# Products of a 128-deep contraction cut into row halves of TensorE and run in pairs

## What is computed

```python
Kf  = einsum('bjd,ed->bje', F, K_w)      # K's product, contraction over d = 128
S   = einsum('bid,bjd->bij', F, Kf)      # scores
out = einsum('bij,ijd->bid', S, W)       # one 64 x 128 matrix W[i] for each row i
out = out + einsum('bid,ed->bie', F, Q_w)  # Q's product, contraction over d = 128
```

## Time and profile before

| What | us |
|---|---|
| median of 3 runs (607.74 to 608.13) | 607.75 |
| the profiled execution, its own time | 608.0 |
| its span | 606.2 |
| PE busy | 597.5 |
| PE weight loads busy | 527.0 |
| VectorE busy | 398.7 |
| ScalarE busy | 401.5 |

### The profile page before, as it was taken

One profiled execution on the slowest core, in us unless ns is written; L12 is line 12 of the kernel. 1 busy time (PEld: TensorE's weight loads), 2 busy tenths in 40 slices (PEclk: granted clock), 3 DMA queues, 4 the chain that ended last, 5 costly groups with the idle time before them and its releaser, 6 DMA issues.

```text
span 606.2 us, 17908 instructions
## 1 busy us (share of the span) xinstructions
PE 597.5 (99%) x7693; PEld 527.0 (87%) x7693; DVE 398.7 (66%) x412; ACT 401.5 (66%) x698; POOL 0.2 (0%) x4
## 2 busy tenths in 40 slices
PE   9999999999999999999999999999999999999995
PEld 7888989889898898988889898898988989889894
DVE  6556757567685665947659475686756768567376
ACT  7978393874938659295692947839387493865830
POOL 0000000000000000000000000000000000000000
PEclk9999999999999999999999999999999999999998
DMA  8543847548575575755647566385755757457177
GB/s 324 239 141 145 322 169 282 199 177 312 189 281 173 212 262 208 280 200 208 246 183 284 204 248 241 140 322 173 285 197 186 304 196 282 173 211 259 66 279 278
DMA packets 29452, 137.60 MB, mean 227 GB/s; under 512 B 3264, under 2 KB 4032, under 8 KB 21312
## 3 DMA queue, kind: packets, MB, share of 16 engines
q1 hardware_dynamic: 20592, 75.38, 31.5%
q10 hardware_dynamic: 8784, 61.08, 28.4%
HBM read 69.34 MB, written 67.11 MB: 225 GB/s over the span
## 4 chain that ended last, share of the span: by engine, by line
PE 98%; DVE 1%; issue 1%; DVEq 0%
PE ps L501 20%; PE ps L440 20%; PE ps L442 19%; PE ps L441 19%; PE ps L527 18%; DVE o_sb L371 1%; PE ps L557 1%; DVEq L46 0%; PE ps L457 0%; PE ps L461 0%; PE ps L459 0%; DVE o_sb L380 0%; DVE f_hi L385 0%
## 5 line engine op out<-in xcount | busy, mean ns | idle before, releaser
L336 DVE TENSOR_TENSOR f_lo<-f_ring,f_hi 128x1024 fp32r<-128x1024 f32 x124 | 151.8, 1224 | 169.6 <-ACT f_hi L214 167.9
L228 ACT ACTIVATE q_out<-ps 128x512 f32<-128x512 f32 x256 | 156.9, 613 | 6.4
L219 ACT ACTIVATE kf<-ps 128x512 f32<-128x512 f32 x256 | 155.9, 609 | 3.4
L371 DVE TENSOR_TENSOR o_sb<-ps,q_out 128x1024 f32<-128x1024 f32 x127 | 145.1, 1213 | 19.3 <-PE ps L527 19.3
L237 ACT ACTIVATE s_t<-ps 128x512 f32<-128x512 f32 x32 | 19.1, 598 | 176.5 <-PE ps L501 176.5
L501 PE MATMUL ps<-f_ring,kf 128*64 128x64 f32 x4096 | 124.1, 222 | 0.4 <-issue 0.4
L501 PEld LDWEIGHTS ps<-f_ring,kf 128*64 128x64 f32 x4096 | 121.6, 138 | 2.9 <-issue 0.8
L527 PEld LDWEIGHTS ps<-s_t,w_sb 64*128 64x128 f32 x2048 | 115.6, 188 | 5.6 <-issue 5.6
L527 PE MATMUL ps<-s_t,w_sb 64*128 64x128 f32 x2048 | 118.6, 274 | 0.0
L440 PE MATMUL ps<-f_hi,k_hi 128*128 128x512 f32 x254 | 100.7, 397 | 0.0
L440 PE MATMUL ps<-f_hi,q_hi 128*128 128x512 f32 x256 | 99.9, 390 | 0.0
(11 more groups left out here) (36 smaller groups left out, 164.3 us busy)
## 6 DMA issues: line engine op xcount, KB each, us to landing
out<-o_sb SPq DMA_DIRECT2D x127, 512.0 KB, 3.5
f_ring<-f_t ACTq DMA_DIRECT2D x58, 1024.0 KB, 4.8
f_ring<-f_t SPq DMA_DIRECT2D x4, 1024.0 KB, 10.4
w_sb<-w SPq DMA_DIRECT2D x1, 2048.0 KB, 18.8
f_ring<-f SPq DMA_DIRECT2D x6, 256.0 KB, 5.1
out<-o_sb SPq DMA_DIRECT2D x2, 256.0 KB, 2.4
f_ring<-f SPq DMA_DIRECT2D x3, 128.0 KB, 2.6
f_ring<-f ACTq DMA_DIRECT2D x1, 128.0 KB, 4.3
```

Source lines behind the costliest of these rows:

```text
L219: nc.scalar.activation(kf[:, c // 2, c % 2 * CK:(c % 2 + 1) * CK, :, :].rearrange("d k h i -> d (k h i)"), ps[:, 2 * c % 8, :], COPY).then ...
L228: nc.scalar.activation(q_out[:, t % 2, :, :].rearrange("d i (h b) -> d i h b", h=2)[:, :, :, at:at + CK], q_bank(t * CHUNKS + c).rearrange ...
L336: nc.vector.tensor_tensor(f_lo[:, v % SPLIT, :], f_unit(v), f_hi[:, v % SPLIT, :].bitcast(F32), ALU.subtract).then_inc(flo_done, 1)
L371: nc.vector.tensor_tensor(o_sb[:, n % OBUF, :, :], ps[:, bank:bank + 2, :], q_out[:, t % 2, :, :].rearrange("d (s m) b -> d s (m b)", s=2) ...
```

## The change

Every product is cut over d into two halves of 64 rows. In a step, a half of one product runs on the lower rows of TensorE and a half of another on the upper rows, pass by pass in turn: first Q's lower half beside K's upper half (`first_halves`), and later K's lower half beside Q's upper half (`second_halves`). The second halves of chunk n are issued after the first halves of chunk n+1. Each pair of passes writes two banks. The second halves wait until the first halves of the same step are complete (`half_done`). The last two chunks are handled as two steps: K's two products side by side, and, after the last scores, Q's two. The first two chunks stay as they were.

K's and Q's products of a chunk now end together, so the users of the slots of `f_hi` and `f_lo` wait for both `q_done` and `k_done`, and TensorE waits for both copies of the chunk four earlier before its first halves. `FILL` is larger.

```diff
-FILL = {2: 58}
-FILL.update((t, 108) for t in range(3, TILES - 1))
-FILL[TILES - 1] = 132
+FILL = {1: 235}
+FILL.update((t, 220 + t % 2) for t in range(2, TILES - 1))
+FILL[TILES - 1] = 284
...
                 act.wait_ge(q_done, 2 * (v - SPLIT) + 2)
+                act.wait_ge(k_done, 2 * (v - SPLIT) + 2)
                 nc.scalar.activation(f_hi[:, v % SPLIT, :], f_unit(v), COPY).then_inc(fhi_done, 1)
...
                 dve.wait_ge(q_done, 2 * (v - SPLIT) + 2)
+                dve.wait_ge(k_done, 2 * (v - SPLIT) + 2)
                 nc.vector.tensor_copy(f_hi[:, v % SPLIT, :], f_unit(v)).then_inc(fhi_dve, 1)
...
-            def k_product(c):
-                three(ps[:, 2 * c % 8, :], k_hi, k_lo, f_hi[:, c // 2 % SPLIT, piece_cols(c)],
-                      f_lo[:, c // 2 % SPLIT, piece_cols(c)]).then_inc(k_done, 1)
+            def products(step):
+                n = min(step, TILES * CHUNKS - LATE)
+                if step < TILES * CHUNKS - LATE:
+                    return (q_of(n), q_done), (k_of(n), k_done)
+                if step == n:
+                    return (k_of(n), k_done), (k_of(n + 1), k_done)
+                return (q_of(n), q_done), (q_of(n + 1), q_done)
...
+            def passes(dst, w_hi, w_lo, c, rows, first):
+                hi = f_hi[rows, c // 2 % SPLIT, piece_cols(c)]
+                lo = f_lo[rows, c // 2 % SPLIT, piece_cols(c)]
+                yield nc.tensor.matmul(dst, w_hi[rows, :], hi, start=first, stop=False)
+                yield nc.tensor.matmul(dst, w_hi[rows, :], lo, start=False, stop=False)
+                yield nc.tensor.matmul(dst, w_lo[rows, :], hi, start=False, stop=not first)
+
+            def first_halves(step):
+                (a, _), (b, _) = products(step)
+                for ins_a, ins_b in zip(passes(*a, lower, True), passes(*b, upper, True)):
+                    pass
+                ins_a.then_inc(half_done, 1)
+                ins_b.then_inc(half_done, 1)
+
+            def second_halves(step):
+
+                pe.wait_ge(half_done, 2 * (step - 1))
+                (a, a_sem), (b, b_sem) = products(step)
+                for ins_b, ins_a in zip(passes(*b, lower, False), passes(*a, upper, False)):
+                    pass
+                ins_b.then_inc(b_sem, 1)
+                ins_a.then_inc(a_sem, 1)
...
-                        pe.wait_ge(kf_copied, n - 3)
+                        k_pieces = 2 if n == TILES * CHUNKS - LATE else 1
+                        pe.wait_ge(kf_copied, n - 4 + k_pieces)
+                        if k_pieces == 1:
+                            pe.wait_ge(q_copied, n - 3)
                     elif t >= 1:
 
                         pe.wait_ge(s_copied_act if c % 2 else s_copied, (t - 1) * 2 + c // 2 + 1)
-                    k_product(n)
-                    if c >= 4:
-                        pe.wait_ge(q_copied, n - 3)
-                    if t < TILES - 1 or c < CHUNKS - LATE:
-                        q_product(n)
+                    first_halves(n)
+
+                    if c >= 1 and n > 2:
+                        second_halves(n - 1)
                     for x in range(FILL.get(t, 0) * c // CHUNKS, FILL.get(t, 0) * (c + 1) // CHUNKS):
                         pe.wait_ge(zeros_done, 1)
+                second_halves(min((t + 1) * CHUNKS - 1, TILES * CHUNKS - LATE))
...
-                    for c in range(CHUNKS - LATE, CHUNKS):
-                        q_product(t * CHUNKS + c)
+                    first_halves(TILES * CHUNKS - LATE + 1)
+                    second_halves(TILES * CHUNKS - LATE + 1)
```

More of the change, by code:

```diff
@@ L92, in build @@
         fhi_done, flo_done = sem("fhi_done"), sem("flo_done")
+        half_done = sem("half_done")
         k_done, kf_copied = sem("k_done"), sem("kf_copied")
@@ L205, in split_first @@
                 wait(act, q_done, 2 * (c // 2 - SPLIT) + 2)
+                wait(act, k_done, 2 * (c // 2 - SPLIT) + 2)
                 nc.scalar.activation(f_hi[:, c // 2 % SPLIT, piece_cols(c)], f_cols(c), COPY).then_inc(fhi_first, 1)
@@ L213, in split_f @@
                 act.wait_ge(q_done, 2 * (v - SPLIT) + 2)
+                act.wait_ge(k_done, 2 * (v - SPLIT) + 2)
                 nc.scalar.activation(f_hi[:, v % SPLIT, :], f_unit(v), COPY).then_inc(fhi_done, 1)
             def copy_kf(t, c):
-                act.wait_ge(k_done, t * CHUNKS + c + 1)
+                n = t * CHUNKS + c
+                act.wait_ge(k_done, n + 1 if n < TILES * CHUNKS - LATE else TILES * CHUNKS)
                 nc.scalar.activation(kf[:, c // 2, c % 2 * CK:(c % 2 + 1) * CK, :, :].rearrange("d k h i -> d (k h i)"),
@@ L222, in copy_q @@
             def copy_q(t, c):
-                act.wait_ge(q_done, t * CHUNKS + c + 1)
+                n = t * CHUNKS + c
+                act.wait_ge(q_done, n + 1 if n < TILES * CHUNKS - LATE else TILES * CHUNKS)
                 if c == 0:
@@ L327, in both_first @@
                 wait(dve, q_done, 2 * (c // 2 - SPLIT) + 2)
+                wait(dve, k_done, 2 * (c // 2 - SPLIT) + 2)
                 if c == 4:
@@ L442, in three, with k_of, q_of @@
                 return nc.tensor.matmul(dst, w_lo[:, :], hi, start=False, stop=True)
-            def k_product(c):
-                three(ps[:, 2 * c % 8, :], k_hi, k_lo, f_hi[:, c // 2 % SPLIT, piece_cols(c)],
-                      f_lo[:, c // 2 % SPLIT, piece_cols(c)]).then_inc(k_done, 1)
+            def products(step):
[5 more added lines that the diff above has]
+                return (q_of(n), q_done), (q_of(n + 1), q_done)
+            def k_of(c):
+                return ps[:, 2 * c % 8, :], k_hi, k_lo, c
+            def q_of(c):
+                return q_bank(c), q_hi, q_lo, c
+            def passes(dst, w_hi, w_lo, c, rows, first):
[17 more added lines that the diff above has]
+                ins_a.then_inc(a_sem, 1)
             def q_product(c):
@@ L467, in project @@
                     n = t * CHUNKS + c
+                    if n == TILES * CHUNKS - 1:
+                        break
                     if n < 2:
```

## The result

The changed kernel takes 614.61 us (median of 4 runs, 613.15 to 615.43), the kernel before 607.75 us beside it. The ratio is 1.0113, with a 95% interval of 1.0088 to 1.0138: slower by 6.9 us, where 2.4% less was predicted. The profiled execution took 613.15 us, with a span of 611.4 us, 5.2 more than before.

A forecast was written before the change was run, and what follows sets the result against it. TensorE's products and the seams between stages were taken as the bound. The span was 606.2 - 12.8 - 2.9 + 0.9 + 0.2 = 591.6 us, and 591.6 + 1.8 - 0.25 gave 593.2 us, range 586 to 601.

The forecast's parts named there:

- The pair's pitch: In the products, a pair of row halves takes 0.2183 us instead of 0.2267 for a full matmul: 12.8 us gained.
- row of 256-column pieces: Pieces at 0.12 us each, 0.013 over their 0.107: the excess is a fixed amount for each matmul, not a slower stream.
- Work costed at nothing because it runs ahead: In TensorE's queue, doubled weight loads and 220 filling waits a tile stay hidden behind the matmuls: no cost.
- The test that was named: Sign of a wrong forecast: products waiting on issue, if the filling waits are dearer than their row.
- The seams: From products to row blocks, now in the same tiling, 0.18 us a tile goes: 2.9 us gained.
- The first tile: Thinner cover makes chunk 5's low part late, 0.7 us lost, and entering the tiling in mid-tile costs 0.2 us.
- The end: The last two Q products have nothing between first and second halves, so `half_done` is waited out: 0.2 us lost.
- Weight loads, splits, copies: In the products, doubled loads are hidden, odd splits keep 0.4 us of slack, bank copies are hidden: no stall counted.
- Rivals 2, 3 and 4: Copies and splits bind, 616 us (0.08); halves don't stream together, 911 us (0.06); weight loads laid bare, 749 us (0.02).
- Rival 1: In the products, the excess stays, a pair takes 0.2267 us, only seams are gained: 606.0 us; chance 0.30.
- Rival 5: In the products, pairs are a little slower than full matmuls, for instance 0.232 us: 614 us; chance 0.11.

The follow-up runs named there:

- the mid-stage change: Kernel before with the change's halves only in the last three chunks of tiles 2 to 15, entering the row tiling inside the products: 613.58 us, ratio 1.0093.
- The pair with small stores: Changed kernel and kernel before, all stores but two writing only the first 128 of 1024 output columns: 603.75 and 604.99 us.

## Why the prediction was wrong

Predicted span 591.6, measured 611.4 us, 19.8 more. By its steps:

- **The pair's pitch** failed, and is the largest part. The step took the 0.005 us of the plain fp32 row blocks as what belongs to the tiling, and the 0.0133 as belonging to the undivided array. Measured is 0.2267 for a pair: the excess is a fixed 0.0133 us of each fp32r matmul. The gain of 12.8 us is 0. The prediction named this as its first rival. Its own row of 256-column pieces already said that the excess goes by matmul, though these pieces are undivided too and could not say whether tiling or data type brings it. A row of the same data type should have outweighed rows of the same tiling.
- **Work costed at nothing because it runs ahead**: the doubled weight loads and the filling waits. Both are indeed hidden while TensorE has instructions. What was not costed is bringing them: 1524 matmuls more in a stream that comes in blocks, behind the stores. That cost 5.9 us in the profiled execution, which was the shortest of the changed kernel's runs, and some 7.5 in the median (614.61 less the 607.15 worked out below). The test that was named, products waiting on issue, is what the profile shows. Its reason was filling waits dearer than their row. They are 0.106 us apart where two follow each other, twice the row, and where they stand behind a late block they lengthen the gap; but with none between, the gap was as long, and without any of them the loss was the same.
- **The seams**: 2.9 us expected, about 2.2 found. The products are 0.09 us shorter in each of 14 tiles, the row blocks 0.95 us in all 16 together. That is 0.15 us a tile instead of 0.18, and only 0.06 of it in the row blocks, where the prediction had placed all of it. The load of the first row block no longer waits for the last product. From the timeline of the changed kernel, where the earlier trace rows had 0.35 us of "issue":

```profile
133.09 0.39 PE L475 MATMUL ps<-f_hi,k_lo 64*128 64x512 f32 x1
133.09 0.97 PEld L578 LDWEIGHTS ps<-s_t,w_sb 64*128 64x128 f32 x13
133.14 0.39 PE L475 MATMUL ps<-f_hi,q_lo 64*128 64x512 f32 x1
133.32 0.82 PE L578 MATMUL ps<-s_t,w_sb 64*128 64x128 f32 x11
```

  0.18 us from the last pair to the row blocks, under a pitch. The page "TensorEngine Tiling (Array Packing)" of the Trainium skill, section "Key Properties", has a change of tiling mode drain TensorE; these rows and the two longer distances of the mid-stage change (0.32 and 0.33 us instead of 0.227) agree with it.
- **The first tile**: 0.9 expected, 1.07 found, with one wait on `f_lo` of 1.0 us where 0.7 was foreseen. The agreement is partly luck: over the profiles this tile's products vary from 25.8 to 27.3 us undivided and from 27.1 to 28.2 in halves.
- **The end**: 0.2 expected, 0.26 found in the late products. Another 0.28 us come after the last matmul (7.18 to 7.46), which the prediction did not have.
- **Weight loads, splits, copies**: right. The load of K's weights at 112.49 us starts together with K's matmul on the same 64 rows, so the rule of the Trainium skill's "TensorE: Matmul & The Clock Gate", section "The mechanism", is not borne out here either. ScalarE is busy for 19.94 us of a tile's products, and no split was waited for after tile 0, though their slack was 0.4 us. Rivals 2, 3 and 4 are out. Rival 1 had the mechanism of the pitch and gave 606.0; it is 8.6 us under the median because it shared the step on instructions. Rival 5's 614 us is near the time, but no pair is slower.

With everything but the blocks as measured, the sum would have been 606.2 - 2.2 + 1.6 + 1.55 = 607.15 us (1.6 is 1.07 + 0.26 + 0.28), 0.6 less than before. The pair with small stores says 1.2, with a first tile 0.33 us longer instead of 1.07.

## What to carry to other kernels

A change that keeps the work and doubles the instructions is not free even when the engine's queue runs ahead: look at where the blocks of the stream end, at the instruction queue's row and at what the DMA engines do then, and look for idle time put down to "issue". Test it by shifting the code with instructions that do nothing before believing a difference of 1% either way. An excess over the streaming time should be read from rows of the same data type before rows of the same tiling.

## What the runs showed of the hardware

- An fp32r matmul costs its columns plus a fixed 13.3 ns (226.7 ns for 512, 120.0 for 256), on all rows or on half of them; bf16 some 2.5 ns (215.9). Two row halves stream fp32r fully at once into two banks: 226.7 ns for a pair.
- TensorE's instructions arrive in 16 KB blocks of 256 through the same DMA engines as data. With these engines full, 16 instructions more or less in one tile moved a kernel by 6.8 us (607.6 to 614.4), and 38 or 100 moved the changed one by up to 2.7. With an eighth of the stores the same 16 moved it by 0.04 us.
- All 131 breaks in TensorE's stream at a block's edge end 1.2 to 1.65 us after the end of a transfer on the instruction queue (twelve profiles). With an eighth of the stores there is none (three profiles).
- Output stores cost the kernel before 2.8 us (607.75 to 604.99) and the changed one 10.9 (614.61 to 603.75). In the profiles 2.0 us of either are the last stores, which are waited for; most of the rest comes through late instructions.
- Entering the row tiling costs 0.20 us in mid-stage (0.32 and 0.33 us instead of 0.227 twice), and 0.15 at the stage's edge (0.09 in the products, 0.06 in the row blocks).
- Two waits in instructions of their own follow each other 0.106 us apart in TensorE's queue, though each is recorded as 0.051.
